# A scatter in every slot of the wide stage, and the expert table made one stage earlier

## The reference, cut to what matters

```python
x = _layernorm(x + _L0_attn_ref(x, ...), axis=-1)          # "taylor"
x = _layernorm(x + _L0_xattn_ref(x, ctx_1024, ...), axis=-1)  # "wide"
x = _layernorm(x + _L0_ffn_ref(x, ...), axis=-1)           # "gelu" experts
x = _layernorm(x + _L1_attn_ref(x, ...), axis=-1)          # "causal"
x = _layernorm(x + _L1_xattn_ref(x, ctx_1024, ...), axis=-1)  # "rotary"
x = _layernorm(x + _L1_ffn_ref(x, ...), axis=-1)           # "swiglu" experts

def _L0_ffn_ref(x, Wr, W1, b1, W2, b2):
    logits = jnp.einsum('nd,ed->ne', xf, Wr)
    probs = jax.nn.softmax(logits, axis=-1)
    w, idx = jax.lax.top_k(probs, TOP_K)
    w = w / jnp.sum(w, axis=-1, keepdims=True)
    gate = jnp.sum(jax.nn.one_hot(idx, E, dtype=xf.dtype) * w[..., None], axis=1)
    for e in range(E):
        h = jax.nn.gelu(xf @ W1[e].T + b1[e], approximate=False)
        y = h @ W2[e].T + b2[e]
        out = out + gate[:, e:e + 1] * y
```

## Time and profile before

| | us |
|---|---|
| median of 3 runs | 2774.44 (2774.1 to 2777.28) |
| the profiled execution | 2774.91 |
| its span | 2773.1 |
| granted TensorE clock, mean | 0.961 |
| PE, DVE, ACT, POOL busy | 91%, 69%, 65%, 52% |

### The profile page before, as it was taken

How to read it: one execution, slowest core, us unless ns; L and a number is a source line. 1 busy time by engine, 2 the same in 40 slices (tenths; PEclk the granted TensorE clock), 3 DMA queues, 4 the chain that set the end, 5 groups by cost and what they waited for, 6 DMA issues and landing times. The chain is left out here.

```text
span 2773.1 us, 62099 instructions
## 1 busy us (share of the span) xinstructions
PE 2528.5 (91%) x19168; PEld 1857.6 (67%) x19168; DVE 1922.4 (69%) x5362; ACT 1813.2 (65%) x5247; POOL 1441.0 (52%) x1854
## 2 busy tenths in 40 slices
PE   8998999999999299996999999959999999699996
PEld 6665787877877289983555555537766666458993
DVE  6884777787777355555778888865788887445655
ACT  6773666666665244445999999949888888623334
POOL 4442334555555645554333333336688888724665
PEclk9998999999999699998999999979999999799998
DMA  8932467777774122214100000000010110001336
GB/s 262 338 105 68 156 216 224 234 223 226 224 214 128 54 65 73 71 56 129 58 11 9 9 9 11 7 25 11 14 33 29 30 30 18 31 29 54 94 92 195
DMA packets 274803, 267.89 MB, mean 97 GB/s; under 512 B 30060, under 2 KB 253561, under 8 KB 274096
## 3 DMA queue, kind: packets, MB, share of 16 engines
q1 hardware_dynamic: 256912, 228.42, 27.2%
q0 software_dynamic: 17280, 34.13, 3.6%
q10 hardware_dynamic: 288, 1.38, 0.2%
HBM read 101.24 MB, written 151.85 MB: 91 GB/s over the span
## 5 line engine op out<-in xcount | busy, mean ns | idle before, releaser
L1274 ACT ACTIVATE causal_exps<-causal_biased,causal_neg_max 128x128 f32<-128x128 f32 x1024 | 325.7, 390 | 23.8 <-DVE causal_neg_max L1579 22.8
L769 POOL TENSOR_TENSOR wide_probs<-wide_exps,wide_inv_sum 128x616 f32<-128x616 f32 x128 | 168.5, 1317 | 305.4 <-DVE wide_inv_sum L1565 295.8
L750 POOL DMA_INDIRECT sorted_x<-send,place_i x240 | 244.2, 1018 | 82.8 <-ACT send L1223 42.7
L1274 ACT ACTIVATE rotary_exps<-banks,rotary_neg_max 128x77 f32<-128x77 f32 x1024 | 249.8, 342 | 20.7 <-DVE rotary_neg_max L1579 20.5
L1825 ACT ACTIVATE gelu_hidden<-banks,gelu_slot 128x256 f32<-128x256 f32 x284 | 116.7, 471 | 159.3 <-PE banks L2002 159.3
L1756 POOL DMA_INDIRECT results<-gelu_tile_out,gelu_dest_i x142 | 140.2, 987 | 142.0 <-DVE gelu_tile_out L1912 119.7
L1524 DVE TENSOR_TENSOR causal_biased<-banks,regions 128x512 f32<-128x512 f32 x256 | 164.0, 682 | 63.2 <-PE banks L1105 60.4
L1130 PEld LDWEIGHTS banks<-first,causal_exps 128*128 128x128 f32 x1024 | 107.2, 141 | 146.8 <-ACT causal_exps L1274 117.3
L1756 POOL DMA_INDIRECT results<-swiglu_tile_out,swiglu_dest_i x142 | 142.4, 1003 | 118.9 <-issue 59.5
L1579 DVE TENSOR_REDUCE rotary_neg_max<-banks 128x4 f32<-128x308 f32 x256 | 121.5, 475 | 105.9 <-PE banks L1119 98.5
L1081 PE MATMUL banks<-wide_folded,wide_probsT 128*128 128x128 f32 x1280 | 187.6, 278 | 6.7 <-DVE wide_z L1509 3.4
(11 more groups left out here) (384 smaller groups left out, 6886.1 us busy)
## 6 DMA issues: line engine op xcount, KB each, us to landing
v_dram<-wide_staged SPq DMA_DIRECT2D x38, 1024.0 KB, 4.5
sorted_x<-blank SPq DMA_DIRECT2D x1, 34848.0 KB, 116.8
sorted_x<-blank SPq DMA_DIRECT2D x24, 1452.0 KB, 8.8
wide_folded<-v_dram SPq DMA_DIRECT2D x128, 256.0 KB
gelu_tile_in<-sorted_x SPq DMA_DIRECT2D x71, 132.0 KB, 2.1
swiglu_tile_in<-sorted_x SPq DMA_DIRECT2D x71, 132.0 KB, 2.1
gelu_back<-results SPq DMA_DIRECT2D x16, 512.0 KB, 8.2
swiglu_back<-results SPq DMA_DIRECT2D x16, 512.0 KB, 5.6
```

The costliest lines, as they stand in the source:

```text
L750: pool.indirect_dma_start(route["sorted_x"], bass.IndirectOffsetOnAxis(ap=r_place_i[:, b % 2, which, n // 2:n // 2 + 1], axis=0), send[:, ...
L769: pool.tensor_tensor(probs[:, half % SLOTS, 0:HH * NK].rearrange("p (k h) -> p h k", h=HH), exps[:, half % EB], inv_sum[:, half % SLOTS].u ...
L1274: last = act.activation(exps[:, (NU * c.c + k) % ES, h], scores[:, h * NK:(h + 1) * NK], ACT.Exp, bias=neg_max[:, k % SLOTS, h:h + 1])
```

## The change

It has two parts. In the wide stage each slot of 16 consecutive ones carries a scatter, where before it was every second of 32; the slot of the first is unchanged, and the rotary stage keeps the old spacing. And the table for the gelu stage is made at the end of the wide stage's list on DVE (with PE's numbers at the end of PE's list), in a part of `region_b` that is free by then; the gelu stage then waits for three things at its start instead of five. The swiglu stage makes its table as before.

```diff
-                    if slot >= 0 and slot % 2 == 0 and slot // 2 < 16:
+                    if late and slot >= 0 and slot % 2 == 0 and slot // 2 < 16:
                         return pair.c // 4, slot // 2
+                    if not late and 0 <= slot < 16:
+                        return pair.c // 4, slot
...
             run(pe, step, STAGES if late or route is not None else 3)
+            if kind == "wide":
+                pe.wait_ge(shifted_done, NU * n_pairs)
+                pe.matmul(chip.banks[:, 1, P:P + TILES], r_ones[:], consts["after"][:, 0:TILES], start=True, stop=True).then_inc(ids_ps, 1)
...
             run(dve, step, STAGES)
+            if kind == "wide":
+                tiles = route["table"]
+                dve.wait_ge(front_ps, FU * n_pairs)
+                dve.memset(tiles["cum"], 0.0).then_inc(table_ready, 1)
+                dve.memset(tiles["jump"], 0.0).then_inc(table_ready, 1)
+                dve.wait_ge(table_ready, 2)
+                dve.wait_ge(base_done, n_pairs // 4)
+                dve.wait_ge(ids_ps, 1)
+                make_table(dve, link, tiles, route["base"], consts["rank8"], chip.banks[:, 1, P:P + TILES], 1156).then_inc(table_ready, 1)
...
-        READY = 5
+        READY = 3 if "table" in w else 5
...
             for done in scattered:
                 sp.wait_ge(done, all_scattered)
-            sp.wait_ge(table_done, 1)
+            if "table" not in w:
+                sp.wait_ge(table_done, 1)
+            row_i = (w["table"] if "table" in w else table)["row_i"]
...
-            link(dve.tensor_scalar(region[:], consts["rank8"], -float(CAPACITY), float(E * CAPACITY), ALU.mult, ALU.add))
...
-            dve.scalar_tensor_tensor(out=row_i[:], in0=ids[0:1], scalar=float(TS), in1=row_f[:], op0=ALU.mult, op1=ALU.add).then_inc(table_done, 1)
-            dve.wait_ge(table_done, 1)
+            if "table" in w:
+                expert_i, row_i = w["table"]["expert_i"], w["table"]["row_i"]
+            else:
+                dve.wait_ge(ids_ps, 1)
+                make_table(dve, link, table, w["base"], consts["rank8"], ids, W).then_inc(table_done, 1)
+                dve.wait_ge(table_done, 1)
+                expert_i, row_i = table["expert_i"], table["row_i"]
...
-            pe.matmul(ids, ones[:], consts["after"][:, 0:NT], start=True, stop=True).then_inc(ids_ps, 1)
+            if "table" not in w:
+                pe.matmul(ids, ones[:], consts["after"][:, 0:NT], start=True, stop=True).then_inc(ids_ps, 1)
```

More of the change, by code:

```diff
@@ L37 @@
 SEND = 2
+TILES = 71
 FILLS = 24
@@ new lines, with table_parts @@
+TABLE = {"region": 8, "count_f": 8, "count_i": 8, "tiles_i": 8, "cum": 32, "jump": 9, "reached": 9 * TILES, "expert_f": TILES, "expert_i": TILES,
+         "row_f": TILES, "row_i": TILES}
+def table_parts(space):
+    parts, at = {}, 0
+    for n, size in TABLE.items():
+        rows = P if n in ("region", "count_f", "count_i", "tiles_i", "cum") else 1
+        v = space[0:rows, at:at + size]
+        at += size
+        if n in ("count_i", "tiles_i", "expert_i", "row_i"):
+            v = v.bitcast(I32)
+        if n == "cum":
+            v = v.rearrange("p (a b) -> p a b", a=2)
+        if n == "reached":
+            v = v.rearrange("p (t e) -> p t e", e=9)
+        parts[n] = v
+    return parts
@@ L1657, in experts @@
         ones = sb("ones", [P, P])
[L1658 to L1664, removed]
+        assert NT == TILES
+        if "table" not in w:
+            table = table_parts(sb("table", [P, sum(TABLE.values())]))
         slot = sb("slot", [P, WR, W])
@@ L1836, in _ @@
             dve.memset(ones[:], 1.0).then_inc(ready, 1)
-            dve.memset(cum[:], 0.0).then_inc(ready, 1)
-            dve.memset(jump[:], 0.0).then_inc(ready, 1)
+            if "table" not in w:
+                dve.memset(table["cum"], 0.0).then_inc(ready, 1)
+                dve.memset(table["jump"], 0.0).then_inc(ready, 1)
             dve.wait_ge(ready, READY)
@@ L1986, in turn @@
                     pe.wait_ge(xT_done, t - 1)
-                if t == 1:
+                if t == 1 and "table" not in w:
                     pe.wait_ge(table_done, 1)
@@ L2153, in build @@
         chip.next_stage()
+        table = table_parts(region_b[:, 16 * P:16 * P + sum(TABLE.values())])
         softmax_attention(chip, "wide", n_seq, X, ctxT_dram, {
@@ L2158, in build @@
             "router": small["g_router"], "gate_bias": None, "tokensT": cut(region_b, 32 * P, [P, 2, 2 * P]), "sorted_x": sorted_x[0], "scattered": dram_sems["scattered"],
-            "turn": 0, "v_dram": v_dram, "cleared": cleared[0], "fills": 1, "meta": meta[:], "base": base[:, 0], "send": send[:], "place_i": place_i[:]},
+            "turn": 0, "table": table, "v_dram": v_dram, "cleared": cleared[0], "fills": 1, "meta": meta[:], "base": base[:, 0], "send": send[:], "place_i": place_i[:]},
             (sorted_x[1], cleared[1], blank[:].rearrange("p a d -> p (a d)")),
@@ L2163, in build @@
         experts(chip, "gelu", n_seq, X, None, sorted_x[0], results, {**dram_sems, "turn": 0}, {
-            "experts": large["g_experts"], "base": base[:, 0], "loaded": (sems["gelu"], 16 * len(expert_parts["g_experts"])),
+            "experts": large["g_experts"], "table": table, "base": base[:, 0], "loaded": (sems["gelu"], 16 * len(expert_parts["g_experts"])),
             "later_loads": [(large["alibi"], weights_dram["alibi"], sems["alibi"])]}, consts)
```

37 lines of the change are left out of this document (21 added, 16 removed).

## The result

The changed kernel takes 2784.96 us (median of 11 executions), the kernel before, on the same chip, 2777.28 us (11): a ratio of 1.0028, 95% interval 1.0018 to 1.0038. It is slower, by some 7.7 us (5 to 11), where 12.0 was forecast. One of its 11 executions took 4635.03 us at a granted clock of 0.824, and the ratio is that of the others. Of the profiled executions the spans are 2773.1 and 2780.4 us.

A forecast was written before the change was run, and what follows sets the result against it. PE was taken to bound the attention, POOL's scatter chain the end. Terms -3.1 (table), +0.6 (tail), +8 and +4.5 (fills), +2 (clock) sum to +12.0 us: 2786.5 us, range 2771.5 to 2797.

The forecast's parts named there:

- Fill at k = 3: Second steps, blocks 0 to 4: ACT's fill waits for the k = 1 scatter, late behind blanking; +8 us (4 to 12).
- fills elsewhere: Fills at k = 1 in blocks 2 to 5 and k = 5 in blocks 0 and 1 wait: +4.5 us (1 to 6).
- cushion of 0.2 us: Block 0's second step: copy to `wide_probsT` ends at 470.3, PE's L1081 needs it at 470.51; landing needed by 468.65.
- The fill's 0.6 us itself is covered: ACT idled 0.75 us before `wide_staged` in block 0's second step, so the fill's own time costs nothing.
- POOL's own time is no bound: covered: A full step's eight scatters fit: POOL's work is 18 of 20.4 us; 1.26 us fits into 1.48 idle.
- The clock, +2 forecast: PE's waits beside the attention lower its clock once in every four or five waits: +2 us (0 to 9).
- Block 7's exponential, +0.6: Tail: the exponential on ACT starts 7.7 us later behind sequence 53's fill, delaying block 7's first scatter: +0.6 us (0 to 1.2).
- The table, -3.1: Gelu stage's start: table made earlier, first load then waits for the last scatter's landing; -3.1 us (-4.7 to -2.5).
- A: Rival: scatters beside the attention land in time, only the ends count: 2772 us; 23%.
- D: Rival: measurable gain, last landing free of the 1 MB load (-4.7) and tail shorter by four scatters (-5): 2765 us; 4%.
- B: Rival: waits exist but are short, half of the 12.5 us, no fall of the clock: 2778 us; 17%.
- C: Rival: long waits that each bring the clock down, 18 us of waits and 9 us of clock: 2799 us; 12%.

The follow-up runs named there:

- four buffers: Changed kernel with four send buffers in the wide stage, not two: 0.9975 and 0.9991 of the kernel before; with the old spacing 0.9982 and 0.9961.
- the run with moved pieces: Changed kernel with the blanking in 22 pieces of 1584 KB, not 24 of 1452 KB, none in the blocks' first steps: 1.0019 of the kernel before.
- the best version: The table's half of the change, the old spacing and four send buffers, against the kernel before: 0.9961 and 0.9982 on two chips.

## Why the prediction was nearly right

**The sign and the mechanism** were right: ACT waits at fills for landed scatters, one to four times for over 1 us in each of blocks 0 to 5, PE behind them, and the table gains 3. The time, 2786.5 forecast, 2784.96 measured, is nearer than its steps deserve: the slowdown is 7.7 us and not 12.0, and it is luck that the kernel before took 2777.28 us on this chip and not the 2774.44 that the forecast started from, which hides 2.8 of the 4.3 us.

- **Fill at k = 3: +8 forecast, and fills elsewhere +4.5.** Of the 8.3 us at pair 30, 5.5 went with the fills' waits when there were four buffers, against 12.5 forecast. The landing was sized well: 469.6 to 471.3 forecast from an issue near 464.0; the issue came at 465.49 and the landing some 6.5 us behind it. What failed is the cushion of 0.2 us. I read in the earlier trace rows that PE's L1081 at 470.51 needs the copy that ended at 470.31. It doesn't; `wide_probsT` has two buffers and PE reads the one filled a slot before, as the rows after show. What PE needs first is `wide_keys`. ACT waited 18 times, 25.3 us in all, and PE lost 5.5 us by it, so ACT may be about 1.1 us late each time (an estimate, 19.8 us over 18 waits). This is where the sum was 7 us too large.
- **Why the landing is late.** I gave it to the blanking, and took it to matter in blocks 0 to 4 only. Blocks 0 and 5 of the run with moved pieces bear out that it matters. But the cut of the `wide_folded` loads took two thirds of the waits away with the blanking in place, and block 5 had a wait of 1.9 us without any: the loads, which I had only named beside the blanking, weigh at least as much. How the two share the waits of blocks 1 to 4 stays open.
- **"The fill's 0.6 us itself is covered", "POOL's own time is no bound: covered".** This was the step that I costed at nothing and that wasn't: 2.7 to 2.8 us with four buffers, when no fill waits, which made up for part of the 7 us. The idle time of 0.75 us ahead of one `wide_staged` was read from one step; ACT's fills now stand twice as often in these steps, and PE waited for `wide_staged` five times.
- **The clock, +2 forecast.** In this profile it went the other way. The granted clock was 1.00 through every wait of a fill beside the attention, and at the attention's end it was low for 3.4 us, not for 3.4 and 6.8, so that the last `wide_z` got 2.0 us back. In none of the twelve profiles is the granted clock low between 285 and 884 us, where the fills' waits of blocks 0 to 4 lie; the falls later differ from run to run and come without any such wait too, as in both kernels with four buffers. The right value was nothing, with some 2 us of spread.
- **Block 7's exponential, +0.6.** Nothing: from block 6's first scatter to block 7's it took 20.40 us (931.48 to 951.88), before 20.37 (924.40 to 944.77). The exponential came the forecast 7.6 us later against the attention's end, and `place_i` was ready 0.03 us before POOL was free for it. What the tail lost instead is 0.4 us, at one scatter of 1.37 us (at 956.22) beside DVE's table.
- **The table, -3.1.** The table alone measured 3.09 us by its rows and 4.4 (1.7 to 7.2) by its ratio. In the changed kernel only 2.0 came: the last scatter landed later against the 1 MB load, its packets still moving at 977 us, 4 us after the issue; three other profiles of the new spacing with two buffers and the early table took 5.15, 5.06 and 4.80 us and not 6.10, so about 1 us of this is the one profile's. "What is next late is the landing" was the right reading.
- **The rivals.** A (all scatters land in time) and D fell with the waits. B (short waits, half of the 12.5 us) was wrong about the landings and right about the size of what they cost; C's falls of the clock did not come.

## What to carry to other kernels

Before packing work that reuses a buffer more closely, compare the time from reuse to reuse with the *longest* completion seen under load, not with the median, and count the buffers first. Then read what the waiting engine's late work really holds up, since most of a wait may be covered (here 20 of 25 us). The buffers are the cure: two more of them removed two thirds of this loss, moving the waiting instruction to another place in the list removed none of it. When a change bundles two parts, time each alone; here one was worth 4 us and the other cost 8 to 12. When an experiment moves a transfer, look up in its trace where the transfer went before reading the time; one here had moved the wrong ones. And a large transfer next to a short one on which a stage's start depends belongs ahead of it: behind it, it only delays the next.

## What the hardware showed beyond that

- An indirect DMA of 66 KB landed 2.3 us after its issue with the DMA engines free (the last five scatters of four buffers with the old spacing), and some 6.5 us while SP's queue kept all 16 busy (the scatter of 465.49 in the changed kernel); the longest seen before was 6.9 us, in the run with moved blanking 7.4. The median of 3.0 us before did not tell which of them a slot gets.
- Delaying a DMA of 1 MB by 4.7 us to free a scatter of 66 KB gave 1.45 us there (last scatter to first load 3.56 us, not 5.01) and took 2.1 us from the next load of 132 KB (5.03 us to `gelu_xT`, not 2.90).
- The second scatter of block 7 starts after 2.11 us in which POOL waited for nothing that the profile shows, in all kernels with two buffers (before, at 947.84, and after, at 954.95), and after 0.30 us in all four profiles with four buffers. This is 1.8 us of the gain of the best version. Why it goes stays open.
